# 64 instead of 60 of 196 edge blocks by one-hots, spread evenly over the steps of a graph network kernel

## The reference

```python
x_j = x[j_idx]; x_i = x[i_idx]                      # 200,000 edges, 12,500 nodes, 32 features
msg = jnp.concatenate([x_i, x_j - x_i], axis=-1)
h = jax.nn.relu(msg @ W1 + b1)                      # 64 -> 64
h = jax.nn.relu(h @ W2 + b2)                        # 64 -> 128
h = jax.nn.relu(h @ W3 + b3)                        # 128 -> 64
m = h @ W4 + b4                                     # 64 -> 32
s = jax.ops.segment_sum(m, i_idx, num_segments=N_NODES)
cnt = jax.ops.segment_sum(jnp.ones((m.shape[0],), m.dtype), i_idx, num_segments=N_NODES)
x = _layernorm(x + s / jnp.maximum(cnt, 1.0)[:, None], axis=-1)
```

## Time and profile before

| | |
|---|---|
| median of 3 runs | 1554.04 us (1551.34 to 1554.89) |
| the profiled execution's own time | 1552.41 us |
| its span, first to last instruction | 1550.6 us |
| busy: PE (TensorE matmul), PEld (weight load) | 1393.1, 958.1 us |
| busy: POOL (GpSimd), DVE (VectorE), ACT (ScalarE) | 1136.0, 853.3, 646.4 us |
| mean granted TensorE clock | 0.93 |

### The profile page before, as it was taken

The page is one execution under the profiler, slowest core; times in us unless marked ns, Lnnn a source line. Parts: engine busy times, 40 slices in busy tenths (PEclk is TensorE's granted clock), DMA queues, the critical chain, the costliest instruction groups (busy, mean ns, idle before and its releaser), DMA issues.

```text
span 1550.6 us, 40086 instructions
## 1 busy us (share of the span) xinstructions
PE 1393.1 (90%) x14162; PEld 958.1 (62%) x14162; DVE 853.3 (55%) x1795; ACT 646.4 (42%) x1009; POOL 1136.0 (73%) x1107
## 2 busy tenths in 40 slices
PE   3356559999999999999999999999999999999867
PEld 2223326676676666666676676666666666667557
DVE  4587615555555555555555555555555555555442
ACT  4253473344334444434344334444333344333354
POOL 4777777777777777777777777777777777777603
PEclk7577769999999999999999999999999999999965
DMA  7534548777777777777777777777777667776401
GB/s 184 167 79 120 111 131 266 228 234 228 224 220 222 220 220 221 227 231 232 229 233 228 228 218 219 215 223 217 231 228 224 206 207 215 225 233 225 93 2 42
DMA packets 197050, 306.49 MB, mean 198 GB/s; under 512 B 84417, under 2 KB 90783, under 8 KB 196280
## 3 DMA queue, kind: packets, MB, share of 16 engines
q1 hardware_dynamic: 161509, 267.12, 53.8%
q0 software_dynamic: 34656, 34.90, 10.4%
q10 hardware_dynamic: 682, 1.85, 0.5%
HBM read 289.68 MB, written 13.92 MB: 196 GB/s over the span
## 4 chain that ended last, share of the span: by engine, by line
POOL 72%; issue 22%; PE 3%; DMA 1%; DVE 1%; DVEq 0%; ACT 0%; SPq 0%; POOLq 0%; ACTq 0%
POOL xj L583 72%; PE ps L1031 3%; DMA sums<-in_src 1%; POOL region L615 0%; DVEq L1347 0%; DMA xj<-z_rows,src_t 0%; DVE region L1355 0%; DVE xmean L1353 0%; PE ps L981 0%; DVE sums L1349 0%; PE ps L801 0%; PE ps L891 0%; PE ps L969 0%; POOL region L609 0%; ACT xj L771 0%
## 5 line engine op out<-in xcount | busy, mean ns | idle before, releaser
L583 POOL DMA_INDIRECT xj<-z_rows,src_t x1043 | 1075.5, 1031 | 318.0 <-issue 318.0
L929 PEld LDWEIGHTS ps<-region,x_p 128*96 128x96 bf16 x6780 | 384.8, 125 | 50.6 <-issue 48.3
L929 PE MATMUL ps<-region,x_p 128*96 128x127 bf16 (+54 forms) x6780 | 390.7, 218 | 4.0 <-DVE region L1303 4.0
L1303 DVE TENSOR_SCALAR region<-region,cst 128x1629 bf16<-128x1629 int16 x480 | 296.6, 679 | 25.0 <-DMA region<-src_rows 24.5
L1322 DVE COPY work<-ps 128x512 f32<-128x512 f32 x188 | 129.1, 686 | 287.1 <-PE ps L969 216.0
L703 ACT ACTIVATE work<-ps,b2s 128x512 f32<-128x512 f32 x392 | 247.9, 683 | 78.3 <-PE ps L953 68.5
L695 ACT ACTIVATE work<-ps,b1s 128x512 f32<-128x512 f32 x196 | 134.7, 687 | 349.8 <-PE ps L873 349.4
L710 ACT ACTIVATE work<-ps,b3s 128x512 f32<-128x512 f32 x196 | 134.7, 687 | 238.3 <-PE ps L961 230.4
L961 PE MATMUL ps<-work,w3s 128*64 128x512 f32 x784 | 215.7, 626 | 18.8 <-ACT work L703 18.8
L953 PE MATMUL ps<-work,w2s 64*128 64x512 f32 x784 | 227.1, 657 | 0.9 <-ACT work L695 0.9
L953 PEld LDWEIGHTS ps<-work,w2s 64*128 64x128 f32 x784 | 60.5, 189 | 168.8 <-issue 113.4
(11 more groups left out here) (160 smaller groups left out, 918.5 us busy)
## 6 DMA issues: line engine op xcount, KB each, us to landing
dstb<-dst_rows SPq DMA_DIRECT2D x196, 252.0 KB
region<-src_rows SPq DMA_DIRECT2D x120, 391.2 KB
region<-src_rows SPq DMA_DIRECT2D x60, 407.2 KB
region<-src_rows SPq DMA_DIRECT2D x60, 403.2 KB
region<-src_rows SPq DMA_DIRECT2D x60, 376.2 KB
region<-src_rows SPq DMA_DIRECT2D x60, 375.8 KB
region<-src_rows SPq DMA_DIRECT2D x60, 374.0 KB
region<-src_rows SPq DMA_DIRECT2D x60, 366.2 KB
```

Source lines behind the costliest of these rows:

```text
L583: pool.indirect_dma_start(out=xj[:, u, j % UT, j // UT, 0:w], out_offset=None, in_=rows, in_offset=bass.IndirectOffsetOnAxis(ap=cols[:, j: ...
L929: chosen = nc.tensor.matmul(ps[0:XP, XBANK[h], lo - h * UE:hi - h * UE], xb[:, a, :], hot[:, q % QN, at + lo:at + hi], start=not begun[h], ...
L1303: nc.vector.tensor_scalar(hot[:, q % QN, 0:CW[c]], spread[:, q % QE, 0:CW[c]], cst[:, C_PID:C_PID + 1], None, ALU.is_equal).then_inc(s_hot, 1)
```

## The change

`SB` becomes 64, so that 132 blocks are gathered instead of 136. The table of steps is made in another way: the sorted blocks take steps 14 to 188, evenly spread, so that the distance from one to the next is 3 in 48 places and 2 in 15 places (mean 2.76). All that is derived from `SB` follows: GpSimd has 1,051 gathers instead of 1,083, and arrays over sorted blocks have 64 rows.

```diff
-SB = 60
+SB = 64
...
-FIRST_SORTED, PERIOD = AHEAD + 4, 3
+FIRST_SORTED, LAST_SORTED = AHEAD + 4, S_N - 8
+SORTED_AT = [FIRST_SORTED + k * (LAST_SORTED - FIRST_SORTED) // (SB - 1) for k in range(SB)]
 for n in range(S_N):
-    k = (n - FIRST_SORTED) // PERIOD
...
+    k = sum(1 for at in SORTED_AT if at < n)
+    STEPS.append(k if n in SORTED_AT else SB + n - k)
```

More of the change, by code:

```diff
@@ L49 @@
 HALF_STEP, PARTS_STEP = 4, 5
-FIRST_SORTED, PERIOD = AHEAD + 4, 3
+FIRST_SORTED, LAST_SORTED = AHEAD + 4, S_N - 8
+SORTED_AT = [FIRST_SORTED + k * (LAST_SORTED - FIRST_SORTED) // (SB - 1) for k in range(SB)]
 for n in range(S_N):
-    k = (n - FIRST_SORTED) // PERIOD
-    sorted_now = n >= FIRST_SORTED and (n - FIRST_SORTED) % PERIOD == 0 and k < SB
-    STEPS.append(k if sorted_now else SB + n - min(max(-(-(n - FIRST_SORTED) // PERIOD), 0), SB))
+    k = sum(1 for at in SORTED_AT if at < n)
+    STEPS.append(k if n in SORTED_AT else SB + n - k)
 assert sorted(STEPS) == list(range(S_N)) and STEPS[-1] == S_N - 1
```

## The result

The changed kernel takes 1554.81 us (median of 20 runs, 1553.46 to 1556.62), the kernel before 1552.85 (20 runs, 1548.87 to 1556.24). The ratio is 1.0015 with a 95% interval of 1.0009 to 1.0021: slower by 2 us in 1553. With so many runs a difference of 0.06% can be told, less than the 0.2% of the prediction. So it moved, where I had forecast no measurable change. It stayed inside the range of 1549 to 1558.

What follows compares the result with a forecast made beforehand. The prediction took TensorE to bound the first two thirds and GpSimd's gathers the last. Sorted steps +26.9, waits -23.2 and centrings -3.1 summed to +0.6 us, giving 1553.0 us, range 1549 to 1558.

Steps and rivals of the forecast that it cites:

- the 0.2% of the prediction: Smallest change of the whole time taken as distinguishable from no change: about 0.2%, 3.1 us.
- the start: Start of the kernel with 64-row fields: every instruction keeps its place, so 0, bounds -0.3 and +1 us.
- Four sorted steps, +26.9: TensorE: four gathered steps of 4.500 us become sorted ones of 11.229, adding 26.9 us.
- The waits for gathers, -23.2: TensorE between steps 16 and 195: all waits for gathers go, saving 23.2 us.
- Gathers at 1.336 us each: GpSimd: each gather with its pause costs 1.336 us, so 32 fewer gathers take off 42.8 us.
- Rival 5: Gathers slow to over 1.36 us beside more one-hots and still come late: 1560 to 1575 us; chance 2%.
- Close pairs, 0: One-hots and window loads of 15 close pairs: cost 0, bounds 0 and a 1 us wait in each.
- Rival 2: Close pairs stall TensorE on late window loads: at 1 us in each of 15 pairs, 1568 us; chance 10%.
- The centrings, -3.1: Four centrings move from steps 194 to 197 to 191 to 194: net -3.1 us, bounds -4.3 and 0.
- The sum, +0.6: All terms together: span 1551.2 us, time 1553.0 us, no difference that can be measured.
- TensorE has slack (rival 1): TensorE takes the four blocks for nothing and GpSimd bounds all the way: 42.8 us off, 1509.6; chance 2%.

## Why the prediction was right, and where it was wrong

The forecast, no difference that can be measured, was wrong: the changed kernel is slower by 2 us, clear of the noise. The account of the two engines held. What failed is one term of the sum, the start, which was put at 0, and the threshold under which a change was called none.

- **Four sorted steps, +26.9.** Right: steps of 11.22 and 4.50 to the end, 10.99 and 4.74 in close pairs. 62 blocks took off 12.2 us between steps 16 and 195 by one profile and 14.5 by the medians (forecast 13.4).
- **The waits for gathers, -23.2.** Right: none left. The two together were forecast at +3.7 us at step 195 from step 16 on; measured 1229.8 - 1225.7 = +4.1, the other 0.4 being small differences of step lengths. Of the 23.2, 19.7 had been waits and the rest the lower clock (granted 0.50 from 1465.9 to 1472.7 us in the kernel before, against 1.00 up to step 195 in the changed one).
- **Gathers at 1.336 us each.** Not a fixed price: 39 us came off for 32 gathers and not 42.8. In the changed kernel a gather came every 1.341 us between 600 and 1000 us and every 1.334 between 1000 and 1300, where it had been 1.320 before. Here it changed nothing. With 60 blocks spread evenly the same fixed price put the last gather 7.6 us too early, with 62 about 10. Rival 5 is out: the pace stayed under 1.36 and no gather was late.
- **Close pairs, 0.** Right, also for 15 in a row. Rival 2 is out.
- **The centrings, -3.1.** Right in sum: the span behind step 195 fell by 3.0, and putting them back costs 3.5. The wait for x was there (0.55 us; a microsecond forecast), TensorE before step 195 was not held up. The chain of line 1422 begins 3.75 us sooner behind step 195's start, and the output, forecast at the same 53.8 us, took 54.2.
- **The start, 0 (bounds -0.3 and +1).** This is the term of the sum that failed. I had counted instructions whose place doesn't change and taken equal time from it. Between the first two profiles it was +1.0, at the upper bound; between the means of three profiles with 60 rows and four with 64 it was +1.2, and by the medians of 20 runs about +1.6. The last store with 64 rows took some 0.35 us longer; the cause of the rest stays open.
- **The sum, +0.6.** Measured +2.1 in the span: +0.6, and 0.4 from the steps, 1.0 from the start, 0.1 from the end. Where two terms of 27 and 23 us nearly cancel, an error of 1.5 us decides whether a change can be seen. That the result lies in the range of 1549 to 1558 says little, since no change at all lies in it too.
- **"0.2% is what can be told".** This failed too, and with it "no difference that can be measured": with 20 runs of each the interval is 0.06% wide to each side.
- **TensorE has slack (rival 1).** Out: the steps keep their length, and weight loads are busy 71% between 600 and 700 us in the changed kernel (68.78% before). So in this kernel the matmul timeline, step against step, was the measure of what TensorE could still take, and a weight-load share of 70% no sign of room.

What 60 to 64 did is to go past the point where both engines end together. From 60 to 62 the time falls by 12 us with the stores split, since GpSimd's end no longer sets it; 3.5 us of this is the centrings' new place. From 62 to 64 it rises by 14.5, most of it because each sorted block in a gathered one's place costs TensorE 6.73 us. 61 and 63 blocks, and where the best number lies, weren't tried.

## What to carry to other kernels

When work is moved between two engines, find for each the time at which it would end alone, and stop at the crossing: the chain that ended last names one engine even if the other is a few us behind. Measure a step's length where nothing waits; with 64 blocks the sum of the steps was right within half a us in 1229, and with 62 within 2.1 us in 1216. A term set to 0 because "nothing moves" still needs a row for its length. And look at what a size that is "only" a row count does to the DMAs: a store of 62 rows in place of 64 took 4.7 us longer.

## What the runs showed of the hardware

- A store's time hung on its number of rows. From the issue of the last store to the loads that wait for it, it was 7.2 us with 62 rows (one profile), 2.5 to 2.6 with 64, 2.2 to 2.3 with 60, and 2.0 and 2.5 behind the second part of a store split into 48 and 14 rows (two profiles). The rule of the Trainium skill that is cited at the kernel with 62 blocks agrees for 62 rows; why 64 rows took longer than 60 it doesn't tell.
- A gather takes longer beside a VectorE instruction with two inputs in SBUF. In the kernel before, VectorE and GpSimd at 636 us, and GpSimd a little later:

```profile
636.45 0.85 DVE L1334 TENSOR_TENSOR region<-iota_s,dst_rel 128x672 f32<-128x672 f32 x1
...
636.57 1.55 POOL L583 DMA_INDIRECT xj<-z_rows,src_t  x1 [0.30 <-issue]
...
639.99 0.94 POOL L583 DMA_INDIRECT xj<-z_rows,src_t  x1 [0.30 <-issue]
```

Between 605 and 990 us, the 57 gathers that overlap line 1334 take 1.31 us in the mean, the 58 beside no VectorE instruction 0.94, and the 77 beside line 1303 alone (one input) 1.01. The 16 beside line 1313 alone, whose one input is in PSUM, take 0.94. The Trainium skill, GPSIMD Engine Reference (Specifications), says that GpSimd shares its SBUF interface with VectorE and meets contention with instructions that have two SBUF inputs; the trace agrees. So GpSimd's pace depends on how VectorE's instructions fall against the gathers. In the kernel before it is one gather in 1.342 us between 600 and 1000 us and in 1.320 between 1000 and 1300, where TensorE waits for gathers; with 60 blocks spread evenly it stays at 1.346 and 1.348, which is most of the 7.6 us by which the last gather was late. Between 1000 and 1300 us the two kernels have nearly the same number of gathers beside line 1334 (46 and 45), but these take 1.21 us in the mean in the kernel before and 1.31 with 60 spread evenly. Why the overlaps are shorter in the one than in the other wasn't tried.
